# Plain fp32 tiles for the first two k steps, smaller first transfers and 22 zero matmuls, in a conditioned feed-forward kernel

## What is computed

```python
def cond(x, weight, ids):                    # x: 8 x 256 x 1024, ids picks one of 8 weights per sequence
    return einsum('bsi,boi->bso', x, weight[ids])

def ffn(xf):                                 # xf: 2048 tokens x 1024
    probs = softmax(xf @ W_router.T)         # 8 experts
    combine = top-2 of probs, normalized, 0 elsewhere
    h = einsum('nd,erd->ner', xf, A_stack) * combine[..., None]       # rank 16
    return xf @ W_base.T + b_base + einsum('ner,eor->no', h, B_stack) * 2.0

x + ffn(cond(x, L0_cond_weight, itok))
```

## Time and profile before

| | before |
|---|---|
| median of 3 runs | 394.69 us (394.64 to 394.70) |
| profiled execution, its time | 394.37 us |
| profiled execution, its span | 392.6 us |
| TensorE busy | 388.7 us (99%) |
| VectorE, ScalarE, GpSimd busy | 302.0, 183.6, 50.0 us |
| read from HBM, written | 64.13 MB, 8.39 MB |

### The profile page before, as it was taken

How to read it: one execution, slowest core, us unless ns; L and a number is a source line. 1 busy time by engine, 2 the same in 40 slices (tenths; PEclk the granted TensorE clock), 3 DMA queues, 4 the chain that set the end, 5 groups by cost and what they waited for, 6 DMA issues and landing times.

```text
span 392.6 us, 5707 instructions
## 1 busy us (share of the span) xinstructions
PE 388.7 (99%) x2185; PEld 332.8 (85%) x2185; DVE 302.0 (77%) x431; ACT 183.6 (47%) x281; POOL 50.0 (13%) x84
## 2 busy tenths in 40 slices
PE   8999999999999999999999999999999999999997
PEld 8888888888888888888888888888888888888886
DVE  4897966789699999974458786778867989998322
ACT  5877734758632444232147666357656224441000
POOL 0101103110002130021130000260000202201110
PEclk9999999999999999999999999999999999999999
DMA  7997875869333145586668767489083302552222
GB/s 263 391 361 281 291 269 125 283 224 334 119 107 27 56 157 169 179 279 206 215 222 275 229 230 251 117 246 387 29 264 117 72 5 81 182 167 80 82 80 80
DMA packets 21979, 73.95 MB, mean 188 GB/s; under 512 B 3344, under 2 KB 3600, under 8 KB 21952
## 3 DMA queue, kind: packets, MB, share of 16 engines
q1 hardware_dynamic: 15984, 55.58, 41.5%
q0 software_dynamic: 5680, 16.96, 14.3%
q10 hardware_dynamic: 288, 1.05, 0.7%
HBM read 64.13 MB, written 8.39 MB: 185 GB/s over the span
## 4 chain that ended last, share of the span: by engine, by line
PE 99%; DVE 0%; issue 0%
PE bank_x L828 30%; PE bank_x L832 16%; PE bank_y L813 9%; PE bank_y L815 9%; PE bank_y L814 8%; PE bank_x L815 8%; PE bank_x L814 8%; PE bank_x L813 8%; PE bank_y L883 2%; PE bank_y L959 2%; DVE out_sb L612 0%; DVE h_hl L549 0%
## 5 line engine op out<-in xcount | busy, mean ns | idle before, releaser
L828 PE MATMUL bank_x<-x_hl,wc_hl 128*128 128x512 f32 x512 | 123.3, 391 | 0.0
L553 DVE TENSOR_TENSOR wc_hl<-raw,wc_hl 128x1024 fp32r<-128x1024 f32 x90 | 108.4, 1220 | 18.5 <-ACT wc_hl L492 18.3
L492 ACT CAST wc_hl<-raw 128x1024 fp32r<-128x1024 f32 x90 | 93.6, 1051 | 56.1 <-DVE raw L557 22.9
L828 PEld LDWEIGHTS bank_x<-x_hl,wc_hl 128*128 128x128 f32 x512 | 94.1, 189 | 18.0
L832 PEld LDWEIGHTS bank_x<-x_hl,wc_hl 128*128 128x128 f32 x512 | 65.9, 191 | 2.6
L832 PE MATMUL bank_x<-x_hl,wc_hl 128*128 128x256 f32 x512 | 66.7, 283 | 0.0
L521 ACT COPY xc_low<-bank_x 128x256 f32<-128x256 f32 x64 | 23.7, 370 | 33.7 <-PE bank_x L832 21.9
L706 DVE TENSOR_TENSOR xp<-bank_x,xc_low 128x256 f32<-128x256 f32 x64 | 26.9, 421 | 15.2 <-ACT xc_low L521 14.1
L814 PE MATMUL bank_x<-x_hl,wc_hl 128*128 128x512 f32 x96 | 37.4, 389 | 0.0
L815 PE MATMUL bank_x<-x_hl,wc_hl 128*128 128x512 f32 x96 | 37.4, 389 | 0.0
L813 PE MATMUL bank_x<-x_hl,wc_hl 128*128 128x512 f32 x96 | 37.4, 389 | 0.0
(11 more groups left out here) (88 smaller groups left out, 505.5 us busy)
## 6 DMA issues: line engine op xcount, KB each, us to landing
raw<-w_cond SPq DMA_DIRECT2D x62, 512.0 KB, 4.7
raw<-w_base SPq DMA_DIRECT2D x24, 512.0 KB, 5.2
out_sb<-x POOLq DMA_DIRECT2D x32, 256.0 KB, 4.7
raw<-x SPq DMA_DIRECT2D x14, 512.0 KB, 4.8
out<-out_sb POOLq DMA_DIRECT2D x28, 256.0 KB, 2.3
raw<-x ACTq DMA_DIRECT2D x2, 512.0 KB, 3.7
raw<-w_cond SPq DMA_DIRECT2D x4, 256.0 KB, 3.5
gate_rows<-compared POOLq DMA_DIRECT2D x16, 64.0 KB, 3.9
```

The source lines that it names most:

```text
L492: nc.scalar.copy(split_dst(key, HI), split_src(key)).then_inc(hi_done, 1)
L553: nc.vector.tensor_tensor(split_dst(key, LO), split_src(key), split_dst(key, HI).bitcast(F32), ALU.subtract).then_inc(lo_done, 1)
L828: return nc.tensor.matmul(ps[:], wc_hl[:, slot_of(s, t), HI, k], x_hl[:, s % 2, k].rearrange("p h n -> p (h n)"), start=(k == 0), stop=stop)
```

## The change

It does four things.

- SP issues W0 in three pieces, (0, 2), (2, 4) and (4, 8), where there were two: the first two of 128 KB.
- The k steps 0 and 1 of output tile 0 are two matmuls on the unsplit fp32 tiles, straight from `raw`, with 256 moving columns, into the lower half of tile 0's bank (L845 of the changed kernel). Wide and narrow matmuls of tile 0 run for k = 2 to 7. The cast of W0's k steps 0 and 1 and their subtraction are gone.
- A new semaphore `start_plain` is raised by the second of them. SP waits for it before it reloads the buffers of X0 and W0.
- The 26 zero matmuls become 21, and one more on the same zeros read as fp32 (L972).

```diff
-SP_MOVES = [(W0, 0, 4), (W0, 4, 8), (W1, 0, 4), (W1, 4, 8)]
-HI_PIECES = [(X0, 0, 2), (X0, 2, 4), (X1, 0, 2), (X1, 2, 4), (W0, 0, 2), (W0, 2, 4), (W0, 4, 8), (W1, 0, 4),
+SP_MOVES = [(W0, 0, 2), (W0, 2, 4), (W0, 4, 8), (W1, 0, 4), (W1, 4, 8)]
+HI_PIECES = [(X0, 0, 2), (X0, 2, 4), (X1, 0, 2), (X1, 2, 4), (W0, 2, 4), (W0, 4, 8), (W1, 0, 4),
              (W1, 4, 8)]
-LO_PIECES = [(X0, 0, 2), (X0, 2, 4), (X1, 0, 2), (X1, 2, 4), (W0, 0, 4), (W0, 4, 8), (W1, 0, 4), (W1, 4, 8)]
-
-START_STEPS = [(0, 0, 8), (1, 0, 4), (1, 4, 8)]
-WARM, WARM_N = 26, 2 * P
+LO_PIECES = [(X0, 0, 2), (X0, 2, 4), (X1, 0, 2), (X1, 2, 4), (W0, 2, 4), (W0, 4, 8), (W1, 0, 4), (W1, 4, 8)]
+
+PLAIN = 2
+START_STEPS = [(0, PLAIN, 8), (1, 0, 4), (1, 4, 8)]
+WARM, WARM_N = 21, 2 * P
...
+        start_plain = sem("start_plain")
...
                     sp.wait_ge(start_lo, piece_count(LO_PIECES, i, tile_steps(i) - 1))
+                    if i in (X0, W0):
+                        sp.wait_ge(start_plain, 1)
...
             def first_cond():
 
+                pe.wait_ge(moved(X0, PLAIN - 1), 16)
+                pe.wait_ge(moved(W0, PLAIN - 1), 16)
+                for k in range(PLAIN):
+                    mm = nc.tensor.matmul(bank_x[0][:, 0:TOK], split_src(START[W0])[:, k], split_src(START[X0])[:, k],
+                                          start=(k == 0), stop=(k == PLAIN - 1))
+                mm.then_inc(start_plain, 1)
                 for t, a, b in START_STEPS:
...
             pe.wait_ge(warm_clear, 1)
             for _ in range(WARM):
                 nc.tensor.matmul(ps_warm[:, 0:WARM_N], h_hl[:, HI, 0, 0:P], h_hl[:, HI, 0, 0:WARM_N], start=True, stop=True)
+            zeros = h_hl[:, HI, 0, 0:TOK].bitcast(F32)
+            nc.tensor.matmul(ps_warm[:, 0:WARM_N], zeros[:, 0:P], zeros, start=True, stop=True)
```

More of the change, by code:

```diff
@@ L828, in wide @@
                 return nc.tensor.matmul(ps[:], wc_hl[:, slot_of(s, t), HI, k], x_hl[:, s % 2, k].rearrange("p h n -> p (h n)"),
-                                        start=(k == 0), stop=stop)
+                                        start=(k == 0), stop=stop,
+                                        skip_group_check=(s == t == 0))
             def narrow(ps, s, t, k, stop=False):
                 return nc.tensor.matmul(ps[:, TOK:], wc_hl[:, slot_of(s, t), LO, k], x_hl[:, s % 2, k, HI],
-                                        start=False, stop=stop)
+                                        start=False, stop=stop, skip_group_check=(s == t == 0))
             def first_cond():
+                pe.wait_ge(moved(X0, PLAIN - 1), 16)
[4 more added lines that the diff above has]
+                mm.then_inc(start_plain, 1)
                 for t, a, b in START_STEPS:
```

## The result

The changed kernel takes 395.34 us (median of 22 runs, 394.72 to 395.70), the kernel before 394.77 in the same comparison (22 runs, 394.52 to 395.55). Its profiled execution took 395.06 us.

What follows compares the result with a forecast made beforehand. TensorE's queue was taken to bound the kernel: two split steps (0.70) go, plain steps (0.88) and leaving fp32 (0.22) come, the zero matmul exchange is even; +0.40 on 394.69 gives 395.1 us, range 394.5 to 396.0.

Steps and rivals of the forecast that it cites:

- rival B: Tile 2: full-price pieces (0.6) plus SP's delay (0.6) make TensorE wait 0.4 us for weights, 395.5 us; chance 11%.
- Zero matmuls (1): Before tile 0: 21 old zero matmuls end at 5.84 us; one fp32 matmul costs 0.44, about 0.86 at the lower clock.
- Entering fp32 (2): Before the fp32 zero matmul: an exposed weight load costs 0.2 us, so that matmul ends at 6.90, as before.
- Leaving fp32 (4): After tile 0's plain k steps: passing back to split matmuls costs 0.22 us at full clock, as at the router.
- The clock (3): Tile 0's two plain k steps: 0.88 us at the upper level, clock low until 7.2, so they end at 7.94.
- The rest of tile 0 (5): Six wide and six narrow matmuls take 2.09 us; tile 1 starts at 10.25 instead of 9.85, +0.40 us.
- SP's queue (7): One more transfer delays later ones up to 0.6 us; tile 2's slack, 0.35 plus TensorE's 0.40, covers it, priced at nothing.

Runs made afterwards that it cites:

- the large second piece: The changed kernel with W0 in two transfers of 128 and 384 KB, (0, 2) and (2, 8): 394.91 us against 394.73 before, ratio 1.0003.

## Why the prediction was right, and where its working was wrong

The number was good: +0.40 us forecast, +0.57 measured, 395.34 inside 394.5 to 396.0, and within 0.2% of before as the likeliest class. **The mechanism was not, and the number was luck.** The forecast time came from TensorE's queue; what happened is rival B, "the weights come last", which had 11%. The rival's places were right: a wait for ScalarE, W2's transfer behind it. Its price, 395.5, is 0.16 from the result, but half of that price was the same 0.40 us of TensorE's queue.

That 0.40 us was nearly all passage: 0.2 for entering fp32 and 0.22 for leaving it. Measured they are 0.00 and 0.03, which leaves +0.01 of the sum. The run with the plain steps and two transfers for W0 agrees with that by its median (0.02 below before), though its interval reaches from 0.16 below to 0.55 above. One error put 0.39 us in, the other left the transfer's 0.5 us out.

Step by step:

- *Zero matmuls (1).* Right in kind. A full fp32 record takes 0.22 us at the upper level, as worked out from the router: L845's weight loads and matmuls last

```profile
L845 PEld LDWEIGHTS bank_x<-raw x4: 187/190/190, 5.9 to 6.5; 128*128 128x128 f32 x4
L845 PE MATMUL bank_x<-raw x4: 379/380/455, 6.0 to 6.7; 128*128 128x256 f32 x4
```

  and the four matmul records start at 5.97, 6.26, 6.48 and 6.69. Two records make one matmul, so 0.43 us; only the first of the four took 0.29, and its weight load was not pulled ahead (it starts at 5.94).
- *Entering fp32 (2): priced at 0.2, measured at nothing.* The last fp32r zero matmul starts at 5.40 and the first fp32 record at 5.51, as far apart as any two of them, and its weight load is pulled ahead to 5.40 (weight port, then the matmuls; start us, us):

```profile
5.40 0.30 PEld L972 LDWEIGHTS bank_y<-h_hl 128*128 128x128 f32 x2
...
5.40 0.28 PE L970 MATMUL bank_y<-h_hl 128*128 128x256 f32 x1
5.51 0.38 PE L972 MATMUL bank_y<-h_hl 128*128 128x256 f32 x1
```

- *Leaving fp32 (4): priced at 0.22, measured at 0.03.* The last plain record starts at 6.69, the second wide matmul at 7.16; 0.22 for the record and 0.23 for a wide matmul would be 7.14. In the profile with two transfers for W0 the same two start at 7.23 and 7.68, 0.00 more than the 0.45. The router's gaps of the earlier trace rows don't come with the number format, at least not at full width. What else differs there is the 32-column weights, four matmuls beside each other; that they are the cause was not tried.
- *The clock (3): taken as fixed at 7.2 us, and it isn't.* L970's row, the zero matmuls of the changed kernel, runs from 279 to 584 ns, where the zero matmuls of the earlier trace rows all take 415 or more:

```profile
L970 PE MATMUL bank_y<-h_hl x21: 279/415/584, 1.2 to 5.4; 128*128 128x256 f32 x21
```

  The pace changed between 5.00 and 5.16 in this execution. The prediction cited the Trainium skill, "TensorE: Matmul & The Clock Gate", section "What's actually happening", that the release moves between executions, and set it aside because three runs lay within 0.06 us. The trace agrees with the page: 7.2 us in one profile, 5.1 in the other. Over the profiles of all the runs the rise lies between about 4.1 us (the large second piece) and 7.2. Three runs were too few, and the time is a poor witness: a TensorE that runs early can only wait longer, as with the fewer zero matmuls, where the time stayed at 395.34.
- *The rest of tile 0 (5).* Tile 1 was to start at 10.25 and started at 9.74. With the two passages at nothing and the early clock it would have been earlier still, but for the hole from 7.16 to 7.98.
- *SP's queue (7): this is the step that failed.* It found the delay of issue (W2's issue at 6.34, forecast up to 0.6 later than 5.77, measured 0.57) and the tightest place, tile 2, with its slack of 0.35. It then covered the delay with 0.40 us by which TensorE would itself be later. TensorE wasn't later; in the profile it was earlier, and there was nothing to cover the delay. With a late clock, too, the sum without its 0.39 us of passages has tile 1 at 9.86, where it was at 9.85 before; that is worked out, not seen. The slack of 0.35 itself was one execution's. And the landing slipped by more than the issue: the cast moved from 11.25 to 12.13, 0.88 us. The DMA engines were less busy than in the kernel before in those microseconds. The windows of the changed kernel (granted clock, DMA share, GB/s at the end) 

```profile
8.00:9.00 1.00, 1.00 (x4) 0.84 (x5) 0.65 (x1) 0.12 (x1) 0.00 (x0) 1.00 0.66 215
9.00:10.00 1.00, 1.00 (x9) 0.93 (x8) 0.47 (x1) 0.89 (x2) 0.00 (x0) 1.00 0.75 285
```

  against those of the kernel before:

```profile
8.00:9.00 1.00, 1.00 (x6) 0.83 (x5) 0.42 (x1) 0.33 (x1) 0.00 (x0) 1.00 1.01 334
9.00:10.00 1.00, 1.00 (x10) 1.00 (x9) 0.67 (x1) 0.36 (x2) 0.00 (x0) 1.00 0.99 377
```

  From 8 to 10 us 0.50 MB were moved instead of 0.71. The prediction's argument against B, that idle DMA engines would let later issues catch up, took their idleness for a reserve, and nothing was caught up. Why they idle isn't shown. It isn't the fifth transfer alone: with four, the same stretch moved 0.52 MB in the profile of the plain steps with two transfers, and 0.56 MB in that of the kernel before with four zeros. So the 0.88 us of these two profiles is in part their chance; what one transfer costs is read from the medians. The Trainium skill's "DMA: Bandwidth & Descriptors", section "Measured (HBM→SBUF, 128 partitions, SWDGE, issued from GpSimd)", gave an estimate of 0.6 us for the split. That is transfer time alone, without SP's delay; the run with the smaller transfers alone shows 0.47 us for both together, and no run here shows the two apart.

Whether it is SP's half microsecond per issue that counts or a fixed price per transfer behind it was not separated. Two more transfers cost 0.88 us, and SP's issues up to W2's come 0.51 to 0.75 apart in the changed kernel, one every 0.58 us, so both would do.

That the whole effect lies ahead of tile 2 can be checked across the kernels whose clock stayed up. From the start of tile 2's first wide matmul to the end of the span it is 380.0 us before (392.6 - 12.65), 380.0 after, 379.9 with the smaller transfers alone (393.6 - 13.66), 380.0 with four pieces (394.0 - 13.98) and 379.9 with W1 whole (392.4 - 12.51). With the four zeros behind tile 3 it is 380.5 (393.9 - 13.38): only there do they come behind tile 2's start, and there they show.

## What to carry to other kernels

A start that has been filled so that TensorE has no gap can look bound by TensorE in one profile while the transfers are only 0.3 us away, or already bind in others. Before a transfer is cut so that its first part lands sooner, add the issue time to everything queued behind it and find the first consumer with less slack than that: here one more transfer cost 0.47 us and two cost 0.88, and a first matmul that came 0.94 us earlier gave nothing back. A slack read from one profile is worth little where the cast of the same load starts at 11.25, 11.93 or 12.28 us with the same number of transfers. And never let a cost of one engine serve as the cover of another's delay unless that cost itself is sure.

## What was unexpected of the hardware

- Matmuls on plain fp32 tiles at full width follow fp32r ones, and are followed by them, almost without a gap (0.00 and at most 0.03 us), where the router's pass through fp32 showed 0.11 and 0.22 us.
- The rise of TensorE's clock from 1.2 to 2.4 GHz at the start came at 7.2 us in one profiled execution and at 5.1 in another, with the same zero matmuls up to then. The earliest was about 4.1 us, with the large second piece.
- A load of 512 KB issued by GpSimd's queue at 6.21 us, beside SP's busy queue, was ready to be cast at 15.10 us, 8.9 us later; SP's loads of that size took 5.8 to 6.5 us in the changed kernel's start. Behind a wait of 3.26 us TensorE's granted clock was 0.52, and in the other kernel with this edit it was 0.50 from 17 to 19 us, behind a wait of 1.85.
